# A graph kernel in which GpSimd gathers every tile of the first layer, and waits twice for each pair of blocks

## The reference

```
h = relu(layernorm(x))
ef  = (relu(edge_attr @ We1 + be1) @ We2 + be2) * sigmoid(edge_weight @ Wt + bt)
msg = relu(concat(h[src], ef) @ Wn1 + bn1) @ Wn2 + bn2
x = x + segment_sum(msg, dst) + h
h = relu(layernorm(x))
x = x + relu(relu((h + segment_sum(h[src], dst)) @ W1 + b1) @ W2 + b2)
```

## Time and profile before

| what | value |
|---|---|
| median of 3 runs | 3862.44 us (3859.89 to 3878.18) |
| profiled execution, its own time | 3848.36 us |
| its span, first to last instruction | 3846.6 us |
| PE busy | 2746.8 us, 71% |
| DVE busy | 1970.9 us, 51% |
| POOL busy | 2069.2 us, 54% |
| ACT busy | 1013.4 us, 26% |
| mean granted PE clock | 0.797 of 2.4 GHz |

### The profile page before, as it was taken

One profiled execution on the slowest core, in us unless ns is written; L12 is line 12 of the kernel. 1 busy time (PEld: TensorE's weight loads), 2 busy tenths in 40 slices (PEclk: granted clock), 3 DMA queues, 4 the chain that ended last, 5 costly groups with the idle time before them and its releaser, 6 DMA issues.

```text
span 3846.6 us, 58359 instructions
## 1 busy us (share of the span) xinstructions
PE 2746.8 (71%) x14587; PEld 1705.2 (44%) x14588; DVE 1970.9 (51%) x4080; ACT 1013.4 (26%) x1000; POOL 2069.2 (54%) x2109
## 2 busy tenths in 40 slices
PE   4877677767677777778777877776663766667667
PEld 3444444444344444435444444443342544455445
DVE  8654555555555555555555555564674333333333
ACT  3332333323233333323233332322231101111112
POOL 7655555555455555555555554545336455555553
PEclk8788888887888788878887887877886767777778
DMA  5433333333333333333334343333213333333331
GB/s 169 123 119 111 113 120 110 111 120 105 117 101 120 110 109 116 120 107 115 112 114 116 104 124 109 114 109 104 79 51 128 99 96 122 123 120 98 111 121 63
DMA packets 234934, 426.49 MB, mean 111 GB/s; under 512 B 86462, under 2 KB 147470, under 8 KB 234542
## 3 DMA queue, kind: packets, MB, share of 16 engines
q0 software_dynamic: 74160, 151.46, 15.3%
q1 hardware_dynamic: 109552, 178.49, 14.1%
q10 hardware_dynamic: 50928, 93.34, 6.8%
HBM read 363.64 MB, written 59.42 MB: 110 GB/s over the span
## 4 chain that ended last, share of the span: by engine, by line
issue 27%; PE 21%; SPq 20%; DVE 13%; another core or an unknown queue 10%; DVEq 7%; DMA 1%; ACT 0%; POOL 0%; ACTq 0%
SPq L486 14%; PE ps L1000 9%; PE ps L900 4%; SPq L482 3%; DVE nodes L1270 3%; PE ps L858 3%; DVEq L1194 2%; PE ps L868 2%; DVEq L1250 1%; DVE arena L1270 1%; DVEq L1267 1%; PE ps L990 1%; DVE big L1220 1%; DVE hot L1225 1%
## 5 line engine op out<-in xcount | busy, mean ns | idle before, releaser
L592 POOL DMA_INDIRECT big<-table,idx x2064 | 2001.8, 970 | 1670.8 <-issue 593.7
L900 PE MATMUL ps<-nodes 128*128 128x500 bf16 x1280 | 433.6, 460 | 324.5 <-DVE nodes L1270 191.4
L858 PE MATMUL ps<-arena,we 128*128 128x512 f32 x784 | 496.0, 762 | 28.5 <-issue 16.2
L713 ACT ACTIVATE big<-big 128x1024 f32<-128x1024 f32 x196 | 207.1, 1057 | 1151.1 <-DVE big L1220 828.3
L1270 DVE TENSOR_SCALAR nodes<-iota_k,win_off,nodes 128x500 bf16<-128x500 f16 x1280 | 461.6, 413 | 0.5 <-issue 0.5
L879 PE MATMUL ps<-hot,big 128*128 128x64 f32 x3136 | 414.2, 288 | 52.8 <-issue 28.2
L879 PEld LDWEIGHTS ps<-hot,big 128*128 128x128 f32 x3136 | 406.0, 208 | 57.6 <-issue 55.7
L1220 DVE TENSOR_TENSOR big<-ps,big 128x1024 f32<-128x1024 f32 x180 | 219.5, 1219 | 354.0 <-issue 287.4
L849 PE MATMUL ps<-arena,we 64*128 64x512 f32 x784 | 258.0, 727 | 199.9 <-DMA arena<-in_ea 187.0
L1267 DVE TENSOR_TENSOR nodes<-iota_b,nodes 128x384 bf16<-128x384 f16 (+1 forms) x492 | 245.5, 499 | 223.0 <-remote 182.6
L1202 DVE TENSOR_TENSOR acc<-ps,acc 128x128 f32 x392 | 114.1, 291 | 458.4 <-remote 398.6
(11 more groups left out here) (152 smaller groups left out, 2604.4 us busy)
## 6 DMA issues: line engine op xcount, KB each, us to landing
arena<-in_ew SPq DMA_DIRECT2D x196, 512.0 KB
arena<-in_ea SPq DMA_DIRECT2D x196, 256.0 KB
counts_d<-arena ACTq DMA_DIRECT2D x192, 245.0 KB
acc<-counts_d ACTq DMA_DIRECT2D x15, 2940.0 KB
big<-table,idx POOLq DMA_INDIRECT x2064
nodes<-table SPq DMA_DIRECT2D x2048, 0.5 KB
table<-big SPq DMA_DIRECT2D x7, 672.0 KB, 3.0
idx<-in_src SPq DMA_DIRECT2D x260, 4.0 KB
```

The source lines that it names most:

```text
L592: pool.indirect_dma_start(to(u, q, t)[0:n], None, table, bass.IndirectOffsetOnAxis(ap=idx[0:n, u, at:at + 1], axis=0))\
L858: i = pe.matmul(p_ef[q], we2[:, :], hid[:, q, :], start=True, stop=True)
L900: m = pe.matmul(to, hots[:, t, :], keys[:, t, :], start=False, stop=True, skip_group_check=True)
```

## The change

Two things change, both in the first layer. SP's fetching is taken out with its buffers and semaphores, and POOL gathers all 8 tiles of every pair; DVE makes all messages in one instruction. With it goes SP's wait for `win_made`, which stood ahead of its first loads for pair 4. And POOL, which waited once ahead of the 8 tiles, now also waits between the first four and the last four, until `agg_mm` has reached n-2, that is until PE has finished the sums of pair n-3 (L882 in PE's own step n). The last two bodies have neither wait. The second layer is as before.

```diff
@@ SyncE
-            def load_pair(at, b, u, first, landed):
+            def load_pair(at, b, u, first):
                 if not first:
                     for q in (0, 1):
-                        sp.wait_ge(gathered[u][q], landed[q])
+                        sp.wait_ge(gathered[u][q], b * (16 * TB))
...
-            def fetch_rows(k, first, last):
-                sp.wait_ge(fetch_idx_loaded[k % 2], k // 2 * 16 + 16)
-                if k >= 2:
-                    sp.wait_ge(pre_made, 2 * FETCHED[k - 2][0] + 2)
-                for p in range(first, last, 4):
-                    _, at = nc.values_load_multi_w_load_instructions(
...
-                    for i in range(4):
-                        sp.dma_start(fetched_rows[k % 2][p + i:p + i + 1, :], table0[bass.ds(at[i], 1), :])\
-                          .then_inc(rows_fetched[k % 2], 16)
-            sp.wait_ge(win_made, NWG)
...
             for b in range(1, NBODY):
                 for u in range(RING):
-                    load_pair(b, b, u, False, [b * (16 * TB) - 16 * fetched_until(u, q, b - 1) for q in (0, 1)])
-                    k, step = divmod(b * RING + u - (FETCHED[0][0] - FETCH + 1), FETCH)
-                    if 0 <= k < len(FETCHED) and step * ROWS < P:
-                        fetch_rows(k, step * ROWS, min((step + 1) * ROWS, P))
...
+                    load_pair(b, b, u, False)
@@ GpSimd
+            def gather_half(b, u, q, last):
+                if last and u == RING - 1:
+                    gather_block(table0, to_rows, u, q, gathered, EDGE_TILES - (NTILE - (2 - q) * TB))
+                else:
+                    gather_block(table0, to_rows, u, q, gathered)
             def gather_body(b, free=False, last=False):
...
                     if not free:
                         pool.wait_ge(ef_mm, b * (2 * RING) + 2 * u)
                     pool.sem_inc(pairs_begun, 1)
-                    if last and u == RING - 1:
-                        gather_last(table0, to_rows, gathered)
-                    elif isinstance(b, int) and b * RING + u in dict(FETCHED):
-                        gather_rest(table0, to_rows, u, dict(FETCHED)[b * RING + u], gathered)
-                    else:
-                        gather_pair(table0, to_rows, u, gathered)
+                    gather_half(b, u, 0, last)
+                    if not free:
+                        pool.wait_ge(agg_mm, b * RING + (u - 2))
+                    pool.sem_inc(pairs_begun, 1)
+                    gather_half(b, u, 1, last)
@@ VectorE, messages
-                    dve.wait_ge(gathered[u][q], (s * NBODY + b) * (16 * TB) + (16 * TB - 16 * fetched))
...
+                    dve.wait_ge(gathered[u][q], (s * NBODY + b) * (16 * TB) + 16 * TB)
+                dve.tensor_tensor(msg[:, u % 2, :, :, :].rearrange("p q t d -> p (q t d)"), p_pre2,
+                                  rows[:, u, :, :, :].rearrange("p q t d -> p (q t d)"), ALU.add).then_inc(pre_made, 2)
```

More of the change, by code:

```diff
@@ L85 @@
 assert sum(SLOTS, ()) == tuple(range(CB))
-FETCH = 11
-ROWS = 12
-FETCHED = tuple((RING + FETCH * (k + 1), k // RING % 2) for k in range(4 * RING))
-assert FETCH * ROWS >= P and P % 4 == 0 and ROWS % 4 == 0 and FETCH % 2 and FETCHED[-1][0] < NPAIR - 2 * RING
-def fetched_until(u, q, b):
-    return sum(n % RING == u and n // RING <= b and half == q for n, half in FETCHED)
-FETCHED_EACH = 2
-assert all(fetched_until(u, q, NBODY) == FETCHED_EACH for u in range(RING) for q in (0, 1))
 NP3 = 3
@@ L468, in _ @@
                   .then_inc(tile_ends_loaded, 16)
-            def load_fetch_indices(k):
-                at = (2 * TB - 1) * FETCHED[k][1]
-                with nc.allow_non_contiguous_dma(reason="one tile's indices in one partition"):
-                    sp.dma_start(fetched_idx[k % 2], src[FETCHED[k][0], :, at:at + 1].rearrange("p a -> a p"))\
-                      .then_inc(fetch_idx_loaded[k % 2], 16)
-            def fetch_rows(k, first, last):
-                sp.wait_ge(fetch_idx_loaded[k % 2], k // 2 * 16 + 16)
-                if k >= 2:
-                    sp.wait_ge(pre_made, 2 * FETCHED[k - 2][0] + 2)
-                for p in range(first, last, 4):
-                    _, at = nc.values_load_multi_w_load_instructions(
-                        fetched_idx[k % 2][:, p:p + 4], engines=(mybir.EngineType.SP,), min_val=0, max_val=N_PAD - 1,
-                        skip_runtime_bounds_check_because="a source index is the number of a node")
-                    for i in range(4):
-                        sp.dma_start(fetched_rows[k % 2][p + i:p + i + 1, :], table0[bass.ds(at[i], 1), :])\
-                          .then_inc(rows_fetched[k % 2], 16)
-            sp.wait_ge(win_made, NWG)
-            for k in (0, 1):
-                load_fetch_indices(k)
             for b in range(1, NBODY):
                 for u in range(RING):
-                    load_pair(b, b, u, False, [b * (16 * TB) - 16 * fetched_until(u, q, b - 1) for q in (0, 1)])
-                    k, step = divmod(b * RING + u - (FETCHED[0][0] - FETCH + 1), FETCH)
-                    if 0 <= k < len(FETCHED) and step * ROWS < P:
-                        fetch_rows(k, step * ROWS, min((step + 1) * ROWS, P))
-                        if (step + 1) * ROWS >= P and k + 2 < len(FETCHED):
-                            load_fetch_indices(k + 2)
+                    load_pair(b, b, u, False)
             sp.wait_ge(sweeps_made, 1)
@@ L599, in gather_pair @@
                     gather_block(table, to, u, q, landed)
-            def gather_rest(table, to, u, half, landed):
-                for q in (0, 1):
-                    gather_block(table, to, u, q, landed, TB, (TB - 1) * q if q == half else None)
             def gather_last(table, to, landed):
@@ L1206, in messages @@
                 dve.wait_ge(pre_mm, n + 2)
-                counted = isinstance(s, int) and isinstance(b, int)
                 for q in (0, 1):
-                    fetched = fetched_until(u, q, b) if counted else FETCHED_EACH
-                    dve.wait_ge(gathered[u][q], (s * NBODY + b) * (16 * TB) + (16 * TB - 16 * fetched))
-                to = msg[:, u % 2, :, :, :].rearrange("p q t d -> p (q t d)")
-                v = rows[:, u, :, :, :].rearrange("p q t d -> p (q t d)")
-                if counted and s == 0 and (b * RING + u) in dict(FETCHED):
-                    k = list(dict(FETCHED)).index(b * RING + u)
-                    one, rest = ((slice(0, D), slice(D, 2 * TB * D)), (slice(2 * TB * D - D, 2 * TB * D), slice(0, 2 * TB * D - D)))[FETCHED[k][1]]
-                    dve.tensor_tensor(to[:, rest], p_pre2[:, rest], v[:, rest], ALU.add)
-                    dve.wait_ge(rows_fetched[k % 2], (k // 2 + 1) * (16 * P))
-                    dve.tensor_tensor(to[:, one], p_pre2[:, one], fetched_rows[k % 2], ALU.add).then_inc(pre_made, 2)
-                else:
-                    dve.tensor_tensor(to, p_pre2, v, ALU.add).then_inc(pre_made, 2)
+                    dve.wait_ge(gathered[u][q], (s * NBODY + b) * (16 * TB) + 16 * TB)
+                dve.tensor_tensor(msg[:, u % 2, :, :, :].rearrange("p q t d -> p (q t d)"), p_pre2,
+                                  rows[:, u, :, :, :].rearrange("p q t d -> p (q t d)"), ALU.add).then_inc(pre_made, 2)
             def pair_hots0(b, u):
```

15 lines of the change are left out of this document (4 added, 11 removed).

## The result

The changed kernel takes 3638.94 us, the median of 6 runs (3632.67 to 3659.5), against 3861.16 us for the kernel before (6 runs): a ratio of 0.9429 [0.9396, 0.9461]. Ratios here compare means and leave out executions over 1.5% above the fastest of their kernel, so a few lie up to 0.3% off the quotient of the medians given beside them. I had said 3769, within 3645 to 3900. The profiled execution took 3632.67 us, 215.7 less than before's 3848.36; its span is 3630.9 us. The mean granted clock of TensorE was 0.797 before and is 0.800 now, so the clock has hardly a part in it.

What follows compares the result with a forecast made beforehand. The prediction took POOL's unbroken run of 8 gathers, which holds back PE's updates, to set the 12.67 us pair cycle. Terms -50 - 4 + 20 - 136 + 105 - 28 = -93 gave 3755 us profiled, 3769 as median, range 3645 to 3900.

Steps and rivals of the forecast that it cites:

- Term 1: SP's queue: without the 2048 one-row DMAs, PE waits less for edge attributes; -50 us, 33 of it in pairs 16 to 39.
- term 2: SP's first loads in the loop no longer stand behind the `win_made` wait; -4 us.
- rival B: POOL's second wait is always already fulfilled and does nothing, runs of 8 gathers stay; 3828 us, chance 0.18.
- Term 3: POOL gathers 16 more tiles at 1.25 us each; +20 us.
- term 4: Long pairs: breaking POOL's run releases PE's held updates, so DVE gets credits 4.4 us earlier in 31 pairs; -136 us.
- term 5: POOL's extra pause at the second wait costs 2.75 us in one of four of the other pairs; +105 us.
- Term 6: Runs of 15 or more gathers, 14 counted: a third of the 83 us they cost at most is saved; -28 us.
- A: Both waits stop POOL in most pairs and its pauses become the bound; slower, 3961 us or 3975 as median, chance 0.14.
- C: PE's held updates are released everywhere and no POOL pause lies on the path; 3664 us, chance 0.13.
- Remote waits of L1155 and L680 under 500: Sign: DVE's and ACT's waits for PE's counts, 857 us together before, fall below 500.
- Attribute waits under 60: Sign: PE's waits for edge attributes fall from 187 us to under 60.
- Long pairs about 16 us: Sign: pairs with 12 or more counting matmuls on PE take about 16 us where they took 20.

Runs made afterwards that it cites:

- e1_no_fetch: The changed kernel without its second wait: SP fetches nothing, POOL gathers all tiles and waits once a pair; 3851.93 us, ratio 0.9968.
- e2_wait_only: The kernel before, SP's fetch kept, with the second wait added between the halves of a pair; 3698.12 us, ratio 0.9574.
- e4_fixed_pause: The changed kernel with ten small memsets on GpSimd between the fourth and fifth gather in place of the second wait; 3606.71 us, ratio 0.9324.
- e16_pause_2_eight: The changed kernel without its second wait, with two memsets on GpSimd ahead of each of a pair's eight gathers; 3681.95 us, ratio 0.9534.
- e11_wait_and_pause: The changed kernel, second wait kept, with five memsets added on GpSimd ahead of each pair's first gather; 3557.29 us, ratio 0.9217.
- e12_pause_4_twice: The changed kernel without its second wait, with four memsets on GpSimd ahead of the first and fifth gather of each pair; 3451.62 us, ratio 0.9064.
- e14_pause_2_six: The changed kernel without its second wait, with two memsets on GpSimd ahead of six of a pair's eight gathers; 3559.88 us, ratio 0.9209.
- e10_pause_2_four: The changed kernel without its second wait, with two memsets on GpSimd ahead of every second gather; 3676.78 us, ratio 0.9488.
- e15_pause_8_once: The changed kernel without its second wait, with eight memsets on GpSimd between the fourth and fifth gather; 3510.48 us, ratio 0.9087.
- e13_fetch_pauses: The kernel before, SyncE's fetch kept, with five memsets on GpSimd ahead of the first and fifth gather of each pair; 3513.99 us, ratio 0.9231.

## Why the prediction was wrong

**Term 1** (-50: -33 in the early pairs, -17 elsewhere) and **term 2** (-4). The early pairs gave -37.4 in the changed kernel and -32.7 in `e1_no_fetch`, without the second wait, so the -33 was right; pairs 0 to 3 gave -3.4 and pairs 4 to 15 -5.1, and the attribute waits are gone. Taken by itself, though, the removal with its 16 more gathers is worth 12 us, not the 34 of terms 1 to 3; this also tests the time of rival B, 3828: measured 3852. The rule of the Trainium skill that another issuing engine saves little (DMA: Bandwidth & Descriptors, Issuing engines are not separate DMA queues) comes close for this removal alone, by its outcome; it doesn't where the second wait stands, 59 us, nor does it tell why.

**Term 3** (+20) can't be told from the rest. The gathers are there, 2080 for 2064.

**Terms 4 and 5** together said -31; pairs 40 to 187, where they mostly act, gave -197.5 (without the second wait, in `e1_no_fetch`, -34.9). The step that failed is above all term 5. It charged a stop of GpSimd in plain pairs as time added to the cycle, +2.75 us in one pair of four, +105; the plain pairs took 246.4 us less. With term 4's 4.4 us a body should have got about 1.7 us shorter. It got 4.3 us shorter by the second wait alone (57.0 to 52.7) and 5.0 in the changed kernel, roughly term 4 with nothing to pay for the stop. Term 4, -136, fits in `e2_wait_only`, whose long pairs gave -100. In the changed kernel they gave +48.9, so there it had the place of the gain wrong too: runs of sixteen, which it expected to become fewer, fall in most of them.

I had read the wait in the earlier trace rows as: POOL's run of 9.9 us and its stop make the cycle of 12.67, so a second stop adds to it. The stop is not added to a fixed cycle. What `e4_fixed_pause` to `e16_pause_2_eight` show is that a GpSimd which is free to run reaches its own wait, stops, and costs over 13 us a pair, while one that is slowed to 11.7 or 11.9 us takes 12.0 or 12.1. The plain pairs of the earlier trace rows weren't at GpSimd's bound; they were at the price of its stopping and starting. The second wait acts like a brake, and an uneven one: it cut the long gaps from 410 to 221 us and left runs of sixteen. It also cut the lateness from 5.4 to 2.9 us; that the brake counts and not the shorter hold rests on `e11_wait_and_pause`, which is later and faster.

**Term 6** (-28) went the other way in its count: runs of fifteen or sixteen rose from 14 to 31.

**The last pairs.** 188 to 194, in the two bodies without GpSimd's waits for PE, take 24.3 us more. I had no term for them. Every other kernel here shows it too, with 151.8 to 172.6 us where the kernel before has 129.3; none was made to tell why.

**The rivals.** A (the pauses become the bound, 3975) had the engine right and the sign wrong: with a pause in every pair POOL is the bound, 49% of the chain, and the time is lower. In the changed kernel itself POOL has 0% of the chain, and plain pairs take 10.36 us, not 15. C (3664) is nearest in time. It is the forecast without term 5, and that much of it was right. It wasn't right as a mechanism, since the updates of L835 are still 2.9 us late, the pauses are there, and the long pairs, its main gain, got longer; that it comes within 25 us is in part luck. The Trainium skill's 26 ns for an increment on a matmul (TensorE: Matmul & The Clock Gate, The cost: per-tile semaphore tail) would have made the second wait worth nothing or less; `e2_wait_only` has it at 4.3%. Lateness doesn't set the time by itself either (3.2 us in the fastest kernel, 0.3 in `e4_fixed_pause`).

**The signs named.** Remote waits of L1155 and L680 under 500: 438. Attribute waits under 60: none listed. Runs of four with gaps of 1.8 to 2.3 us: there, but fewer than those of eight and more. Long pairs about 16 us: 22.5. I had watched the runs and not the sum of GpSimd's long gaps, which was the sign that told.

**What stays open.** Why a free GpSimd pays two microseconds a pair. The held updates are the candidate: its own wait is among what is held, and afterwards it sends a long run, which holds the others. But no kernel here has updates that come out at once beside a GpSimd that runs free, so that is argued and not shown. A second candidate is TensorE itself, which issues slowly late in a long run. In the run of sixteen above, the last sums of L832 come one by one:

```profile
1919.77 1.36 PE L832 MATMUL ps<-hot,big 128*128 128x64 f32 x10
...
1922.93 0.22 PE L832 MATMUL ps<-hot,big 128*128 128x64 f32 x1 [1.17 <-issue]
1925.06 0.22 PE L832 MATMUL ps<-hot,big 128*128 128x64 f32 x1 [1.91 <-issue]
...
1928.60 0.27 PE L832 MATMUL ps<-hot,big 128*128 128x64 f32 x1 [2.56 <-issue]
```

Between 586 and 2350 us such idle time of PE adds up to 179 us before, 331 in the changed kernel, 264 in `e1_no_fetch`, 82 in `e12_pause_4_twice` and 9 in `e16_pause_2_eight`. It doesn't follow the time, and no run takes it apart from the rest. The mean granted clock was 0.83 in `e12_pause_4_twice` and 0.80 in the changed kernel; how much of the time between them that makes wasn't separated. It can't be all: `e11_wait_and_pause` reaches 0.9217 at 0.808, `e14_pause_2_six` 0.9209 at 0.826. Nor was a pace tried between 11.3 and 11.7 us.

## What to carry to other kernels

Where an engine works in bursts ahead of its consumers and is then stopped by its own wait, price a pause there not as time added to its cycle but by whether it still stops afterwards: add up its long idle stretches and compare its own time for a step with the step's measured time. If the measured step is well above it (here 14.3 us for 10.0), slow the engine to just under what the others need and measure a few steps of pace. And measure the halves of a change apart before crediting either: here one half was worth 12 us alone and 59 behind the other. A gain's place among the steps can move while its sum over a body stays, so test a term on the sum.

## What the runs showed of the hardware

- A matmul's semaphore update is late beside a run of GpSimd's indirect gathers, by 5.4 us in the mean for L882 before (136 found). Breaks of 0.63 us ahead of every second gather leave it at 5.2 us (`e10_pause_2_four`, 124 found), ahead of every gather at 0.0 (`e16_pause_2_eight`, 126 found). One break of 2.68 us a pair leaves 0.3 us (`e4_fixed_pause`, 138 found), one of 2.16 us 3.5 (`e15_pause_8_once`, 143 found).
- Twelve one-row DMAs with their register loads take SyncE 11.2 us in the mean in the kernel before and 8.4 where GpSimd pauses 1.39 us after every four (`e13_fetch_pauses`).
- A chain of five memsets of 128 x 120 on GpSimd takes 1.24 us, four take 0.98, and two make the gap between gathers 0.63 us instead of 0.30.
- The kernel's time is not monotone in the work given to GpSimd: 1.7 us of added memsets a pair (own time 10.0 to 11.7) take 9% off it, and 0.9 us more (12.6) give half of that back.
